# Four projected time steps computed in the waits of earlier blocks, and low halves made by VectorE, in a two-layer decoder kernel

## The reference, cut to what matters

```
x = _layernorm(x + _L0_attn_ref(...))                    # "ln0" in the kernel
x = _layernorm(x + _L0_xattn_ref(x, side, ctx_1024))     # two int8-style quantised products q0, q1, then "ln1"
x = _layernorm(x + _L0_ffn_ref(x, ...))                  # feed-forward, block "ffn", then "ln2"
...
x = _layernorm(x + _L1_xattn_ref(ctx_1024, x, ...))      # a selective scan over ctx_1024, independent of x until its gate
```

```
dt_low, Bm, Cm = jnp.split(x_dbl, [dt_rank, dt_rank + d_state], axis=1)   # dt_rank = 16, d_state = 16
dt = jnp.einsum('brl,dr->bdl', dt_low, dt_proj_w)
dt = jax.nn.softplus(dt + dt_proj_b[None, :, None])
A = -jnp.exp(A_log)
state = state * exp(d * A) + (d * u) * b ;   y = sum_n state * c
```

## Time and profile before

| | |
|---|---|
| Median of 3 executions | 3909.66 us (3907.2 to 3920.04) |
| Profiled execution: time, span | 3927.57 us, 3925.8 us |
| TensorE matmul busy | 3475.6 us (89%) |
| VectorE busy | 3141.7 us (80%) |
| ScalarE busy | 1623.4 us (41%) |
| GpSimd busy | 1296.5 us (33%) |
| Granted TensorE clock, mean | 0.939 of 2.4 GHz |

### The profile page before, as it was taken

The page is one execution under the profiler, slowest core; times in us unless marked ns, Lnnn a source line. Parts: engine busy times, 40 slices in busy tenths (PEclk is TensorE's granted clock), DMA queues, the critical chain, the costliest instruction groups (busy, mean ns, idle before and its releaser), DMA issues. The chain is left out here.

```text
span 3925.8 us, 41107 instructions
## 1 busy us (share of the span) xinstructions
PE 3475.6 (89%) x15146; PEld 1472.0 (37%) x15406; DVE 3141.7 (80%) x2717; ACT 1623.4 (41%) x2201; POOL 1296.5 (33%) x509
## 2 busy tenths in 40 slices
PE   5777779989999979998999979999999979967998
PEld 1222233334333443334333443434333443424444
DVE  5899479797999769797999769787999769795333
ACT  5666353225556353225655343224655343213001
POOL 3232204352444304352344304352344314361000
PEclk9788999999999989989999989989899989978999
DMA  6688402221333302221333302221233302110322
GB/s 231 242 305 294 162 11 81 74 68 56 100 99 112 131 11 81 73 67 57 99 97 110 134 11 74 79 68 57 89 107 103 132 22 73 60 38 17 105 97 73
DMA packets 105430, 382.94 MB, mean 98 GB/s; under 512 B 14224, under 2 KB 27920, under 8 KB 102800
## 3 DMA queue, kind: packets, MB, share of 16 engines
q1 hardware_dynamic: 83632, 342.57, 25.6%
q10 hardware_dynamic: 21600, 37.73, 3.4%
HBM read 290.80 MB, written 64.32 MB: 90 GB/s over the span
## 5 line engine op out<-in xcount | busy, mean ns | idle before, releaser
L300 PE MATMUL ps<-r,ring 128*128 128x512 bf16 (+1 forms) x2015 | 770.3, 383 | 20.5 <-DMA ring<-wsplit 8.7
L297 PE MATMUL ps<-xr,ring 128*128 128x512 bf16 x1525 | 596.1, 391 | 2.7
L301 PE MATMUL ps<-xr,ring 128*128 128x512 bf16 x1515 | 590.8, 390 | 1.2
L297 PE MATMUL ps<-r,ring 128*128 128x512 bf16 (+3 forms) x1338 | 526.3, 394 | 38.8 <-DVE xc L1125 20.7
L301 PE MATMUL ps<-r,ring 128*128 128x512 bf16 (+1 forms) x1353 | 531.3, 393 | 1.1 <-issue 0.2
L1176 POOL TENSOR_TENSOR hh<-hh,bc 128x2048 f32<-128x2048 f32 (+1 forms) x72 | 309.8, 4303 | 454.8 <-DVE hh L1084 454.8
L1176 POOL TENSOR_TENSOR bc<-bc 128x2048 f32<-128x2048 f32 (+1 forms) x64 | 279.8, 4372 | 353.0 <-DVE bc L1084 353.0
L1176 POOL TENSOR_TENSOR r<-r,bc 128x2048 f32<-128x2048 f32 (+1 forms) x56 | 239.9, 4284 | 314.4 <-DVE r L1084 314.4
L1084 DVE TENSOR_TENSOR_SCAN hh<-da,hh 128x2048 f32<-128x2048 f32 x72 | 317.8, 4414 | 0.6
L1125 DVE TENSOR_TENSOR xc<-xc,ps 128x512 f32<-128x512 f32 x176 | 119.5, 679 | 225.9 <-PE ps L301 220.5
L300 PEld LDWEIGHTS ps<-r,ring 128*128 128x128 bf16 (+1 forms) x2040 | 196.2, 96 | 244.0 <-issue 9.5
(11 more groups left out here) (275 smaller groups left out, 6520.9 us busy)
## 6 DMA issues: line engine op xcount, KB each, us to landing
ring<-wsplit SPq DMA_DIRECT2D x216, 768.0 KB, 4.2
r<-wstream SPq DMA_DIRECT2D x54, 768.0 KB, 7.2
ring<-wsplit SPq DMA_DIRECT2D x76, 512.0 KB, 4.0
wsplit<-ring SPq DMA_DIRECT2D x38, 768.0 KB, 5.0
da<-r ACTq DMA_DIRECT2D x360, 63.9 KB, 2.1
wsplit<-r SPq DMA_DIRECT2D x14, 768.0 KB, 5.1
r<-wstream SPq DMA_DIRECT2D x19, 512.0 KB, 6.4
r<-xT SPq DMA_DIRECT2D x7, 1024.0 KB, 4.9
```

The lines of the kernel that those rows point to most:

```text
L297: mm = pe.matmul(out, w_hi, x_hi, start=start, stop=False)
L300: pe.matmul(out, w_hi, x_lo, start=False, stop=False)
L301: return pe.matmul(out, w_lo, x_hi, start=False, stop=stop)
```

## The change

What the old `norm_and_steps` did for the steps is divided over the four blocks, all of which now share one `ScanInputs` object with the banks 2 to 5 for the step products.

- ln0: after the variances TensorE makes the four step products; 8 instead of 20 `keep_busy` matmuls follow. After its factors ScalarE takes steps 0 and 1 out of PSUM (Identity with the bias, into `dtx`).
- q0: ScalarE takes steps 2 and 3 while VectorE works out the smoothing factors, and both halves' magnitudes (SBUF to SBUF, 128x1024) before it waits for the row scales. TensorE waits for the four steps before its first transposes.
- q1: ScalarE works out the two exponentials before it waits for the row scales. VectorE takes the positive part in place, half 0 behind the reciprocal of the row scales, half 1 ahead of the wait for the broadcast scale.
- ln1: TensorE spreads rows 0 to 3 between the means and the variances. ScalarE starts with a table load for Ln and both logarithms, and its factors load no table for Ln again. VectorE: sums, centred, four rows, both totals, scaled. GpSimd only builds the spreading matrix.
- ffn: VectorE starts with the four low halves; TensorE waits for them ahead of `gate(0)`, behind `spread_dt(0)` and `spread_dtx(0)`.

```diff
+    def take_step(self, act, j):
+        act.wait_ge(self.dtp, j + 1)
+        act.activation(self.dtx[:, j, :], self.dt_bank(j), ACT.Identity, bias=self.dtb[:, j:j + 1]).then_inc(self.step_in, 1)
+    def magnitudes(self, act, i):
+        act.wait_ge(self.step_in, (i + 1) * self.half)
+        act.activation(self.dt[:, self.part(i), :], self.dtx[:, self.part(i), :], ACT.Abs).then_inc(self.absd, self.half)
+    def positive_part(self, dve, i):
+        part = self.part(i)
+        dve.wait_ge(self.absd, (i + 1) * self.half)
+        dve.tensor_scalar(self.dtx[:, part, :], self.dtx[:, part, :], 0.0, None, ALU.max).then_inc(self.zread, self.half)
...
@@ hidden_and_scan, TensorE, then VectorE
                 spread_dtx(0)
+            if tiles and not gated:
+                pe.wait_ge(xsplit, KM)
             if tiles:
                 gate(0)
...
+            if tiles and not gated:
+                for c in range(KM):
+                    low(dve, xlo[:, c, :], k.xr[:, c, :]).then_inc(xsplit, 1)
             if blocks:
                 inputs(0)
...
@@ LayerNorm.factors
-        act.wait_ge(self.sq, 4)
-        act.preload_act_table(ACT.Ln)
+        if not loaded:
+            act.wait_ge(self.sq, 4)
+            act.preload_act_table(ACT.Ln)
...
@@ layer_norm (ln0), TensorE, then ScalarE
             norm.variances(pe)
-            keep_busy(k, pe, 0, 20)
+            if steps:
+                for j in range(J1):
+                    steps.dt_product(pe, j)
+            keep_busy(k, pe, 0, 8 if steps else 20)
...
             norm.factors(act)
+            if steps:
+                for j in range(J1 // 2):
+                    steps.take_step(act, j)
...
@@ norm_and_steps (ln1)
-            s.dt_product(pe, 0)
-            s.dt_product(pe, 1)
             norm.means(pe)
-            s.dt_product(pe, 2)
-            s.dt_product(pe, 3)
+            for r in range(GRP):
+                s.spread_row(pe, r)
             norm.variances(pe)
-            for r in range(2 * GRP):
+            for r in range(GRP, 2 * GRP):
                 s.spread_row(pe, r)
...
-            for j in range(J1):
-                s.magnitude(act, j)
-            norm.squares(act)
-            norm.factors(act)
-            for i in range(2):
-                s.exponential(act, i)
+            act.preload_act_table(ACT.Ln)
             for i in range(2):
                 s.logarithm(act, i)
+            norm.squares(act)
+            norm.factors(act, True)
...
             s.build_spread(pool)
-            for half in range(2):
-                for pair in range(2):
-                    pool.wait_ge(norm.out, 2 * half + pair + 1)
-                    part = lambda region: region[:, 2 * pair:2 * pair + 2, half * HT:(half + 1) * HT]
-                    pool.tensor_tensor(part(k.ffn_xlo), part(k.xr), part(high(k.xr)), ALU.subtract)
...
             norm.sums(dve)
-            s.positive(dve, 0)
-            s.positive(dve, 1)
             norm.centred(dve)
-            s.positive(dve, 2)
-            s.positive(dve, 3)
             for r in range(GRP):
                 s.dve_row(dve, r)
-            norm.scaled(dve)
             for i in range(2):
                 s.total(dve, i)
+            norm.scaled(dve)
...
@@ quant_linear: VectorE behind the reciprocal of the row scales, and ahead of the wait for the broadcast scale
+            if not hidden:
+                steps.positive_part(dve, 0)
...
+            if not hidden:
+                steps.positive_part(dve, 1)
...
@@ quant_linear: ScalarE behind its table warm-up, and behind the smoothing of the weights; TensorE
+            if hidden:
+                for j in range(J1 // 2, J1):
+                    steps.take_step(act, j)
...
+            for i in range(2):
+                if hidden:
+                    steps.magnitudes(act, i)
+                else:
+                    steps.exponential(act, i)
...
             keep_busy(k, pe, 0, 20 if hidden else 10)
+            if hidden:
+                pe.wait_ge(steps.step_in, J1)
...
@@ sequence
+                    steps = ScanInputs(k, 1, None, (0, 1), {"dt": W_FFN}, (2, 3, 4, 5), ready=True)
```

More of the change, by code:

```diff
@@ L336, in __init__ @@
             k.sem(f"prep{which}_{n}") for n in ("tap", "conv", "xs", "ysplit", "ts_mm", "bcs_mm", "ts_in", "bcs_in", "tsplit")]
+        self.step_in = k.sem(f"prep{which}_step_in")
         self.dtp, self.absd, self.zread, self.spexp, self.spln, self.dtsum, self.spread, self.row_mm, self.row_in = [
@@ L819, in hidden_and_scan @@
         gate_mm, up_mm, th, silu, hid, weighted = [sem(n) for n in ("gate_mm", "up_mm", "th", "silu", "hid", "weighted")]
-        hidlo, down, taken = [sem(n) for n in ("hidlo", "down", "taken")]
+        hidlo, xsplit, down, taken = [sem(n) for n in ("hidlo", "xsplit", "down", "taken")]
         dt_mm, dtx_mm, decay, others = [sem(n) for n in ("dt_mm", "dtx_mm", "decay", "others")]
@@ L1221, in squares, with factors @@
                 act.activation(self.half(k.xr, h, pair), self.half(k.xc, h, pair), ACT.Square).then_inc(self.sq, 1)
-    def factors(self, act):
+    def factors(self, act, loaded=False):
         k = self.k
-        act.wait_ge(self.sq, 4)
-        act.preload_act_table(ACT.Ln)
+        if not loaded:
+            act.wait_ge(self.sq, 4)
+            act.preload_act_table(ACT.Ln)
         for h in range(2):
@@ L1256, in scaled, with layer_norm @@
                                   ALU.mult).then_inc(self.out, 1)
-def layer_norm(nc, k, tag, parts, slots_end, last, store=None, load=None, split=None, ranges=(), residual=None, summed=False):
+def layer_norm(nc, k, tag, parts, slots_end, last, store=None, load=None, split=None, ranges=(), residual=None, summed=False, steps=None):
     with ExitStack() as ctx:
@@ L1306, in _, with norm_and_steps @@
             norm.scaled(dve)
-def norm_and_steps(nc, k, tag, parts, slots_end, last):
+def norm_and_steps(nc, k, tag, parts, s, slots_end, last):
     with ExitStack() as ctx:
         norm = LayerNorm(k, tag, parts, k.xr, [k.ps[:, 4 + h, 0:HT] for h in range(2)], [k.ps[:, 6 + h, 0:HT] for h in range(2)])
-        s = ScanInputs(k, 1, None, (0, 1), {"dt": W_FFN}, (0, 1, 2, 3), (0, 1, 2, 3), ready=True)
+        s.row_banks = (0, 1, 2, 3)
         blk = ctx.enter_context(nc.Block())
@@ L1356, in _, with quant_linear @@
             norm.sums(dve)
-            s.positive(dve, 0)
-            s.positive(dve, 1)
             norm.centred(dve)
-            s.positive(dve, 2)
-            s.positive(dve, 3)
             for r in range(GRP):
                 s.dve_row(dve, r)
-            norm.scaled(dve)
             for i in range(2):
                 s.total(dve, i)
-def quant_linear(nc, k, tag, kt, xt, wt, w_range, hidden, slots_end, last):
+            norm.scaled(dve)
+def quant_linear(nc, k, tag, kt, xt, wt, w_range, hidden, steps, slots_end, last):
     with ExitStack() as ctx:
@@ L2374, in sequence @@
                 with cleared():
+                    steps = ScanInputs(k, 1, None, (0, 1), {"dt": W_FFN}, (2, 3, 4, 5), ready=True)
                     layer_norm(nc, k, "ln0", k.ps[:, 0:KM, :], W_FFN, last, ranges=[(k.guw_range, k.guw), (k.ctx_range, k.ctxT)],
[L2376 to L2379, removed]
+                               residual=k.next_x, steps=steps)
+                    quant_linear(nc, k, "q0", KM, k.xr, k.guw, k.guw_range, True, steps, W_FFN, last)
+                    quant_linear(nc, k, "q1", 2, k.xc[:, 0:2, :], k.ctxT, k.ctx_range, False, steps, W_FFN, last)
+                    norm_and_steps(nc, k, "ln1", k.xc, steps, W_FFN, last)
                 with cleared():
```

## The result

The changed kernel takes 3876.2 us (median of 5; 3873.2 to 3883.72), the kernel before 3920.04 us beside it (5 executions, 3907.2 to 3922.62). The ratio is 0.9891 with a 95% interval of 0.9869 to 0.9914: 34 to 51 us of 3920, about 43. The forecast of 3867.5 us stood on the median of three executions, 3909.66 us; two more, of 3921.47 and 3922.62 us, moved that median to 3920.04 us, so a gain of 42 us would now read 3878 us. Two later comparisons of the same pair gave 0.9881 (0.9849 to 0.9914) and 0.9872 (0.9850 to 0.9894). The profiled execution takes 3876.2 us with a span of 3874.4 us, 51.4 us less than the span before.

What follows compares the result with a forecast made beforehand. VectorE was taken to bound ln1, 28.0 us on average. Savings of 9.7 + 3 x 10.7 = 41.8 us, taken as 42, with moved work free, gave 3867.5 us; range 3852 to 3886 us.

Steps and rivals of the forecast that it cites:

- ln1 on VectorE: New ln1: VectorE's sums, centred, rows, totals and scaled take 15.87 us at full clock, saving 9.7 us.
- The factors: In ln1, TensorE and ScalarE have the factors ready at 13.4 us, just when VectorE is ready for `scaled`.
- GpSimd out of VectorE's way: In ln1, without GpSimd's low halves beside it, `scaled` takes 2.50 instead of 4.17 us.
- Covers: ScalarE's work moved into ln0, q0 and q1 is hidden in waits; margins in q0 and q1 are 0.2 us each.
- Start of ffn: VectorE's low halves end at 3.0 us, covered by TensorE's step matmuls; first inputs stay at 4.09 us.
- Rival A: Shorter idleness keeps 2.4 GHz into ffn (1.1 us a sequence), later means run at full clock: 3857 us; chance 0.12.
- The last three sequences: ln1 there, with slow means and variances: 18.1 instead of 28.8 us, saving 10.7 us three times.
- ln0, the step that failed: In ln0, 12 step matmuls replace 12 of TensorE's 20 `keep_busy` matmuls, all with 512 columns, at no cost.
- signs named for being wrong: Over 1 us wait for ScalarE before `scaled`, rounding over 0.3 us behind the reciprocal, or later blocks changing several microseconds.
- Rivals B: TensorE and ScalarE's chain ends ln1 at the lower clock: 3891 us, or 3880 if in two sequences; chance 0.19.
- C: The ffn block falls out of step, its array longer at 1.2 GHz: slower, 3917 us; chance 0.03.
- D: Thin covers in q0 and q1 are overrun and engine order costs the rest: no gain, 3910 us; chance 0.04.

Runs made afterwards that it cites:

- e3: The changed kernel with VectorE's totals behind `scaled` in ln1, as they stood before: 3889.84 us, ratio 0.9896.
- e5: The changed kernel with both exponentials at the start of ln1 instead of in q1: 3881.02 us in one execution.
- e1: The kernel before, with the low halves made by VectorE at the start of ffn and no steps moved: 3913.92 us, ratio 0.9961.
- e2: The changed kernel with the low halves back on GpSimd in ln1: 3894.52 us, ratio 0.9911.
- e4: The changed kernel with 20 matmuls that nobody reads behind the last spread row of ln1: 3875.71 us, ratio 0.9864.
- e8: The changed kernel with 20 unread matmuls behind ln1's spread rows, and ln0's eight in pairs ahead of each step product: 3880.02 us, ratio 0.9880.

## Why the prediction was right, step by step

- *ln1 on VectorE.* Predicted 15.87 us at full clock, measured 15.60. Sums and centred, rows, totals and scaled each came within 0.15 us. e3 shows that the totals fill the wait for the factors.
- *The factors* were ready 11.6 us into the block, not at 13.4: I had taken the spread rows between means and variances at the upper bound of 2.91 us, and they take 1.14. So VectorE ends the block with 1.5 us in hand, and e5 used nearly all of it at no cost.
- *GpSimd out of VectorE's way.* Shown by e1 and e2 in both directions: `scaled` goes from 4.17 to 2.48 us without GpSimd's low halves, and from 2.49 to 4.18 us with them.
- *Covers.* All held with the margins of the prediction (0.40 and 0.19 us against 0.2 and 0.2). Nothing of ScalarE's work moved into ln0, q0 and q1 is on the path: in ln0 it ends 1.1 us ahead of VectorE. The table load in q1 takes 1.28 us with the exponentials at once behind it, as the prediction's row said.
- *Start of ffn.* Predicted 4.1 us, measured 4.10. Rival A's first half, that 5 us of idleness would keep the clock, is refuted by the trace (the step matmul takes 2.04 us behind 5.44 us of idleness). Its mechanism is shown by e4, and by e5 without added matmuls.
- *The last three sequences* were mis-sized: 18.1 us predicted, 15.6, 15.6 and 17.3 measured, 6 us more gain in all. I had carried the slow means of the kernel before over to the new block. Where the means are slow after, the variances still take 3.72 us, so that VectorE doesn't wait for the factors, and ln1 is 15.6 + 1.7 and not 18.1 us. Over the three traces of the changed kernel ln1 took 15.6 us in ten of twelve sequences. This is the second half of rival A, though its reason was wrong for ln0, where twelve of the twenty matmuls now have 16 rows. Why the means met the lower clock in three of four sequences before and in two of twelve after was not settled. The step products that stood ahead of them in ln1 are a candidate: the means are slow in six of eight sequences of the two traces that have them there, and in 14 of 48 of the others. No run moved them alone.
- *ln0, the step that failed.* "12 step matmuls replace 12 of the 20 `keep_busy` matmuls, all with 512 columns: nothing." They cost 1.3 us in three of twelve sequences of the changed kernel, because the clock is sometimes down behind them and the eight left over take 3.5 us. Over all traces with this ln0 it is 17 of 40 sequences of 14.2 us or more, and none of eight in the two traces (before, e1) whose twenty matmuls have 128 rows. So the exchange brings the lower clock into ln0; which property of the step products does it stays open, since in e8 the clock fell too, only later.
- *Total.* 42 us predicted, about 43 measured. That they lie so close is in part luck: ln1 gives 48 us in the trace where 42 were summed, ln0 takes 2.6 us back, the interval is 34 to 51 us, and the profiled executions differ by 51 us. The forecast time is 8.7 us too low, which is the baseline and not the sum. Of the signs named for being wrong, one was touched: the later blocks changed by 6.8 us, more than a few, but less than they differ between traces of unchanged code (14 us). ln1 itself lies just under the 15.9 to 18 us that were to show. Rivals B, C and D did not occur: ffn takes 703.8 us against 703.6.

## What to carry to other kernels

When one engine ends a block, write its list down with durations from rows and put the work that waits for nobody into the waits of that list: the order alone was worth 3.3 us of 19 here. Work moved into another block is free only up to the wait there. An overrun can come with more than its length (0.7 us of it went with 3 us a sequence in one execution; the cause of the rest isn't shown). And matmuls that take the place of as many others can still bring the lower clock: it came into ln0 in 17 of 40 sequences with the step products there, and in none of eight without. Judge changes of a few microseconds by the stage in the trace, and then ask the total: three variants won 5 to 10 us in their stage and nothing that the total could show.

## What the runs showed of the hardware that was not expected

- Eight identical 128-row matmuls take 1.90 or 3.5 us behind 12 matmuls of 16 rows, in the same program (3.2 to 3.6 us, once 2.6, over all traces with this ln0). With two of the eight ahead of each three, ln0 had one length, 13.36 us, in all four sequences, and the clock fell at its end in two.
- The 20 such matmuls in 5.4 us of idleness kept 2.4 GHz into the next block in four sequences of four (2.73 us to the first inputs instead of 4.10).
- Without them, the first step matmul took 1.09, 1.09 and 1.15 us behind 4.02 us of idleness and 2.04 us behind 5.44 us, in one program (e5).
- Stages of the same code come in a few lengths. Over the three traces of the changed kernel q0 takes 26.6 or 28.2 us, and q1 17.8, 18.6 or 18.9 to 19.1 us. Which one occurs was not settled.
- Two subtractions from SBUF on VectorE take 3.02 us beside two on GpSimd; four alone take 2.50 us. Here sharing is slower than not sharing. The Trainium skill (SBUF — State Buffer, "Who interferes with whom") says that a VectorE instruction with two SBUF inputs contends with a GpSimd instruction that reads SBUF, and this trace agrees.
